# Weighted sums of two attention steps issued together, in every second step

## Chip, cores and metric

The kernel runs on one core of one Trainium2 chip. The metric is the device time of one execution in microseconds; lower is better. TensorE is the matmul engine, VectorE, ScalarE and GpSimd (POOL in the rows) the elementwise ones, SP the queue that issues the transfers.

## What is computed

One transformer layer (16 heads of 16, width 256) followed by a layer of experts, both behind a layernorm, on 4 sequences of 2048 tokens. The part around the change is the attention:

```python
scores = jnp.einsum('bhqd,bhkd->bhqk', q, k) / jnp.sqrt(jnp.float32(HD))
allowed = (idx % STRIDE == 0)[:, None] | (idx[:, None] == idx[None, :])
scores = jnp.where(allowed, scores, -jnp.inf)
attn = jax.nn.softmax(scores, axis=-1)
o = jnp.einsum('bhqk,bhkd->bhqd', attn, v)
```

Only every eighth token (256 of 2048) attends to all keys; each other token sees itself alone, so its result is its own value vector. The attention matrix is therefore computed for 256 queries and 2048 keys a head.

## The kernel before

`build_steps` (lines 81 to 416) writes out one list of steps, `STEPS`. Each engine walks the whole list and issues its own part of each step, so the list is the order of work on every engine, and semaphores tie the engines together. For each of the 4 batches there is a projection stage and an attention stage; behind the last one comes a tail. Next to each stage run "blocks" of the two MLPs (M: the layer's MLP with GELU, F: the experts' with ReLU), eight items a block.

**Attention stage.** Heads go in 8 pairs, keys in 8 groups of 256 (`KK`), which makes 64 steps (`STEPS_B`) a batch. Step 0's scores are issued at the end of the projection stage, so `attention(b)` begins with step 1. `step(s)` (line 309) puts:

- `scores(s)`, "sc" (lines 1720 to 1730): four matmuls of 128 keys by 256 queries for two heads, into PSUM banks 0 and 1. Before them TensorE waits for the exponential of step s - 1, which reads these banks (`bank_free`, line 1631). ScalarE then takes the exponential of 128x1024 elements into one of two `prob` buffers (lines 1146 to 1158); from step 2 on it waits for the weighted sum of step s - 2, which reads the same buffer (line 1156).
- `maxima(s)`, "mx" (lines 1706 to 1715): two matmuls of 512 columns into banks 2 and 3 for the maxima of a head pair that comes later; VectorE reduces them (line 1428). Before them TensorE waits for the reduction of the maxima before (line 1629). They run 12 ahead (`LEAD`), so that steps 52 to 63 have none.
- `weighted(s - 1)`, "at" (lines 1731 to 1741): `prob` times `vals` for two key tiles and two heads, accumulated in bank 4 over the 8 steps of a head pair. Each of the four products is in fp32, with an output of 32 partitions at its own quarter of the array, and the trace shows two matmuls for each: eight a step. It waits for the exponential of its own step. Behind the last one of a head pair stands "or": VectorE copies bank 4 to `oraw` (line 1452).
- `turns(s)` and `moves(s)`: turning `oraw` and the maxima, and transfers for later work.

**Blocks beside it.** A loop over quarters (line 320) puts one quarter of an item after the steps that are due. Part 0 is three up matmuls of 512 columns ("up", 0), part 1 three more ("up", 1), with a fourth in F blocks (line 1809), part 2 six down matmuls of 256 columns ("dn", 0), part 3 "ev" and six more ("dn", 1). `three` (line 1548) issues these products in groups of three (lines 1550 to 1552). ScalarE has GELU or ReLU (lines 1191, 1193) and a rounding copy (line 1199) per item, POOL a subtraction (line 1049). VectorE has, beside the maxima, subtractions for turned tiles (line 1495), the layernorms and the choice of the expert (lines 1342 to 1359).

Batches 0 and 3 have 16 items in the attention stage, so 64 quarters for 64 steps: one quarter a step, and at the stage's start two steps back to back twice (steps 2 and 3, steps 5 and 6). Batches 1 and 2 have 24 items: one quarter behind an odd step, two behind an even one. This is the line that says it:

```python
            ahead = min(2, quarter // 2) if len(blocks) == 2 else 0
            while s < STEPS_B and s * 4 * n <= (quarter + ahead) * STEPS_B:
                step(s)
                s += 1
```

Three places outside wait for the last weighted sum of a batch: SP (line 913) and ScalarE (lines 1124 and 1169).

Of the kernel before, what the change touches and what calls it, by code (L numbers as in the profile page):

```python
# [42 lines left out]
STEPS_B = PAIRS * KK  # L43
# [33 lines left out]
def blocks_of(what, b):  # L77
    return [k for k, s in enumerate(PHASE) if s == (what, b)]


def build_steps():
# [5 lines left out]
    def down(half):  # L87

        if len(pending) <= LAG:
            return  # L90
        i = pending[0]
        put(("dn", i, half))
        if half == 1:
            pending.pop(0)
            if i % FT == FT - 1:
                put(("sum", i // FT))
# [44 lines left out]
    def after(k, f, at):  # L141

        if k < 0:
            return
        what = BLOCKS[k][0]
        if f == 2:
            put(("la", k))
        if what == "M" and f == at:
            put(("lb", k))
        if what == "F" and f in (3, 4):  # L150
            put(("lf", k, f - 3))
        if f == (at + 1 if what == "M" else 5):
            put(("st", k))

    def rows_in(k, f, at):

        if f == (3 if k == 1 else 0) and BLOCKS[k][0] == "M":
            put(("ld", k))
        if f == at and PHASE[k][0] != "tail" and k + 2 < len(BLOCKS) - 1 and BLOCKS[k + 2][0] == "F":
            put(("ld", k + 2))  # L160
# [3 lines left out]
    def mx(b):  # L164
        m = mine[0]
        if m < PAIRS * MPP:
            put(("mx", b, m // MPP, m % MPP))
            mine[0] += 1
            if m % MPP == MPP - 1:
                put(("ng", b, m // MPP))  # L170
# [89 lines left out]
    def attention(b):  # L260
        blocks = blocks_of("attention", b)
        n = FT * len(blocks)

        def scores(s):
            put(("sc", b, s // KK, s % KK))

        def maxima(s):
            if mine[0] < s + LEAD + 1:
                mx(b)

        def weighted(s):
            if s >= 0:
                put(("at", b, s // KK, s % KK))
                if s % KK == KK - 1:
                    put(("or", b, s // KK))

        alone = []

        def turns(s):
            p, kk = s // KK, s % KK  # L280
            if p and kk == 1:
                alone.append([("ot", b, p - 1)])
            if kk == 4 and p + 1 < PAIRS:
                alone.insert(0, [("mt", b, p + 1), ("mtd", b, p + 1)])

        def turned_out(s, taken):

            if alone and (alone[0][0][0] == "mt" or len(blocks) == 2 or s % KK in (0, 7) or not taken):
                for one in alone.pop(0):
                    put(one)  # L290
                return True
            return taken

        def moves(s):
            p, kk = s // KK, s % KK
            if kk == 1 and p and p + 2 < PAIRS:
                put(("kld", b, p + 2))
            if s == 4:
                put(("ldg", b))
            if b + 1 < B:  # L300
                if s == 6 * KK + 1:
                    for q in range(XB):
                        put(("ldx", b + 1, CHUNKS[q]))
                for at, one in ((53, ("pa", b + 1, CHUNKS[0])), (55, ("pb", b + 1, CHUNKS[0])), (58, ("pt", b + 1, CHUNKS[0])),
                                (60, ("pa", b + 1, CHUNKS[1]))):
                    if s == at:
                        put(one)

        def step(s):

            scores(s)
            maxima(s)
            weighted(s - 1)
            turns(s)
            moves(s)

        s, hook = 1, []

        places = [(0, 2, 4, 7)] * 2 if len(blocks) == 2 else [(0, 2, 3, 7), (0, 1, 3, 7), (1, 2, 4, 7)]
        for quarter in range(4 * n):  # L320
# [5 lines that stand above are left out]
            i, part = FT * blocks[0] + quarter // 4, quarter % 4  # L326
            k, f = i // FT, i % FT
            ready = k + 1
            at = places[k - blocks[0]]
            if part == 0:  # L330
                put(("up", i, 0))
            elif part == 1:
                put(("up", i, 1))
                pending.append(i)
                after(k - 1, f, 4)
                rows_in(k, f, 6)
                if f == at[2] + 1:
                    put(("pick", ready, 1))
                if f == at[2] + 2:
                    put(("pick", ready, 3))  # L340
            elif part == 2:
                down(0)
                hook = dict(zip(at, ([("tn", ready, 0)], [("tn", ready, 1), ("xw", ready)], [("ga", ready)], [("pi", ready)]))).get(f, [])
                taken = bool(hook)
                if hook and hook[0][0] == "pi" and alone and alone[0][0][0] == "mt":
                    turned_out(s, False)
                for one in hook:
                    put(one)
                if not hook:
                    taken = turned_out(s, False)  # L350
            else:
                put(("ev", i))
                turned_out(s, taken)
                down(1)
                if f == at[2]:
                    put(("pick", ready, 0))
                if f == at[2] + 1:
                    put(("pick", ready, 2))
        assert s == STEPS_B and not alone
        weighted(STEPS_B - 1)  # L360

    def tail(b):
# [53 lines left out]
    for b in range(B):  # L416
        mine[0] = 0
        projection(b)
        attention(b)
# [1428 lines left out]
```

## Time and profile before

| | |
|---|---|
| median of 3 runs | 1447.2 us (1447.17 to 1449.56) |
| the profiled execution | 1452.35 us |
| its span, first to last instruction | 1450.6 us |
| TensorE (PE) busy | 1404.0 us, 97% |
| VectorE (DVE) busy | 846.5 us, 58% |
| ScalarE (ACT) busy | 721.7 us, 50% |
| GpSimd (POOL) busy | 649.0 us, 45% |
| weighted-sum matmuls, line 1739 | 2048, mean 391 ns |
| exponentials, line 1157 | 256, mean 1023 ns |
| reductions of the maxima, line 1428 | 256, mean 1223 ns |

In rows of the timeline the first number is the start in us from the span's start, the second how long the row lasts. PE is a matmul, PEld a load of weights. Ends of matmuls are modelled and reach over the next one's start; starts are what to go by. A row of several instructions ("x8") lasts from the first start to the last end. In brackets stands the idle time of the engine before it and what ended that. "L1713" is line 1713 of the kernel. The four attention stages last from 163.9 to 310.4, 482.2 to 662, 830.8 to 1010.6 and 1183.9 to 1330.1 us.

### The profile page before, as it was taken

To read this page: it belongs to the slowest core of one execution; us is meant where nothing else is said; L and a number is where in the kernel's file an instruction comes from. 1 tells how busy PE (TensorE), PEld (TensorE's weight loads), DVE (VectorE), ACT (ScalarE), POOL (GpSimd) and SP (SyncE) were. 2 spreads that over 40 slices of the span, in tenths; PEclk is the share of its full clock that TensorE was granted. 3 is DMA by queue.
4 is the path that set the end of the run, shared out by engine and by line. 5 is a ranking of instruction groups with operands and counts; after the bars stand their busy time and mean duration, and the time that the engine had idled before them with its cause. 6 is when DMAs were issued, how large, how long until landed. Compare 5 with 4: busy or idle time off the path is not lost.

```text
span 1450.6 us, 26449 instructions
## 1 busy us (share of the span) xinstructions
PE 1404.0 (97%) x10167; PEld 1063.0 (73%) x10167; DVE 846.5 (58%) x1792; ACT 721.7 (50%) x1071; POOL 649.0 (45%) x533
## 2 busy tenths in 40 slices
PE   6889999999999999999999999999999999999997
PEld 4778655678888766668888866666888875557996
DVE  7747676636656666555647575763566556762332
ACT  3444555554444555554444555555344455555442
POOL 4554321338754414145865431333776441132755
PEclk9899999999999999999999999999999999999999
DMA  7464123215561222212682213220556212310100
GB/s 251 158 177 103 50 51 66 55 41 190 186 163 44 58 59 50 55 44 81 205 211 69 76 31 79 55 55 16 166 188 166 87 38 50 79 26 23 52 15 30
DMA packets 91393, 130.50 MB, mean 90 GB/s; under 512 B 8314, under 2 KB 68180, under 8 KB 88148
## 3 DMA queue, kind: packets, MB, share of 16 engines
q1 hardware_dynamic: 91268, 128.82, 32.2%
q8 instruction: 81, 1.33, 0.4%
q14 instruction: 44, 0.36, 0.1%
HBM read 68.08 MB, written 60.57 MB: 89 GB/s over the span
## 4 chain that ended last, share of the span: by engine, by line
PE 78%; DVE 11%; POOL 5%; issue 2%; ACT 1%; DMA 1%; SPq 0%; POOLq 0%; DVEq 0%; ACTq 0%
PE ps L1550 19%; PE ps L1551 16%; PE ps L1552 16%; PE ps L1739 9%; PE ps L1728 6%; PE ps L1713 4%; DVE mx L1428 3%; PE ps L1787 2%; DVE stats L1302 2%; PE ps L1775 2%; PE ps L1809 2%; POOL rows L1034 2%; PE ps L1745 1%; PE ps L1671 1%; DVE xn L1390 1%
## 5 line engine op out<-in xcount | busy, mean ns | idle before, releaser
L1428 DVE TENSOR_REDUCE mx<-ps 128x2 f32<-128x1024 f32 x256 | 311.1, 1223 | 189.9 <-PE ps L1713 188.3
L1157 ACT ACTIVATE prob<-ps 128x1024 f32<-128x1024 f32 x256 | 261.8, 1023 | 139.1 <-PE ps L1728 138.8
L1049 POOL TENSOR_TENSOR hid1l<-gel,hid1h 128x512 fp32r<-128x512 f32 x85 | 111.3, 1310 | 207.1 <-ACT hid1h L1199 206.9
L1049 POOL TENSOR_TENSOR hid2l<-gel,hid2h 128x512 fp32r<-128x512 f32 x85 | 111.4, 1311 | 201.6 <-ACT hid2h L1199 201.6
L1049 POOL TENSOR_TENSOR hid0l<-gel,hid0h 128x512 fp32r<-128x512 f32 x86 | 112.5, 1308 | 194.2 <-ACT hid0h L1199 194.2
L1191 ACT ACTIVATE gel<-ps,cols 128x512 f32<-128x512 f32 x128 | 88.1, 688 | 181.0 <-PE ps L1552 169.9
L1739 PE MATMUL ps<-prob,vals 128*32 128x256 f32 x2048 | 163.6, 391 | 0.0
L1193 ACT ACTIVATE gel<-ps 128x512 f32<-128x512 f32 x128 | 76.5, 598 | 170.6 <-PE ps L1809 170.6
L1728 PE MATMUL ps<-qslot,kslot 50*128 50x256 f32 x1024 | 128.9, 330 | 1.8 <-ACT prob L1157 1.8
L1728 PEld LDWEIGHTS ps<-qslot,kslot 50*128 50x128 f32 x1024 | 76.2, 184 | 66.5 <-issue 46.9
L1713 PE MATMUL ps<-kslot,qslot 48*128 48x512 f32 x512 | 102.3, 410 | 3.5 <-DVE mx L1428 3.0
L1028 POOL TENSOR_TENSOR rstd<-vare,mhalf 128x4 f32<-128x4 f32 x47 | 48.3, 1027 | 76.7 <-DVE vare L1316 75.0
L1739 PEld LDWEIGHTS ps<-prob,vals 128*32 128x32 f32 x2048 | 40.3, 108 | 57.6 <-issue 50.6
L1034 POOL TENSOR_SCALAR rows<-rows,mv,rstd 128x256 f32<-128x256 f32 x60 | 73.6, 1233 | 0.0
L1550 PE MATMUL ps<-turned0h,wih 128*128 128x512 f32 x128 | 58.7, 459 | 0.0
L1550 PE MATMUL ps<-turned1h,wih 128*128 128x512 f32 x128 | 57.1, 446 | 0.0
L1495 DVE TENSOR_TENSOR turned1l<-ps,turned1h 128x512 fp32r<-128x512 f32 x32 | 22.1, 692 | 59.7 <-ACT turned1h L1164 59.7
L1713 PEld LDWEIGHTS ps<-kslot,qslot 48*128 48x128 f32 x512 | 46.5, 185 | 11.3 <-DVE mx L1428 7.4
L1199 ACT ACTIVATE hid0h<-gel 128x512 fp32r<-128x512 f32 x86 | 54.1, 629 | 1.3
L1550 PE MATMUL ps<-turned1h,w1h 128*128 128x512 f32 x128 | 54.2, 423 | 0.0
L1199 ACT ACTIVATE hid2h<-gel 128x512 fp32r<-128x512 f32 x85 | 53.5, 630 | 1.3
L1199 ACT ACTIVATE hid1h<-gel 128x512 fp32r<-128x512 f32 x85 | 53.4, 629 | 1.3
(244 smaller groups left out, 3956.5 us busy)
## 6 DMA issues: line engine op xcount, KB each, us to landing
k_d<-kst SPq DMA_DIRECT2D x192, 128.0 KB
kslot<-k_d SPq DMA_DIRECT2D x64, 384.0 KB
xin<-in_L_attn_x SPq DMA_DIRECT2D x32, 256.0 KB, 4.0
rows<-xs_d SPq DMA_DIRECT2D x16, 512.0 KB, 6.0
y_d<-rows SPq DMA_DIRECT2D x15, 512.0 KB, 3.1
rows<-y_d SPq DMA_DIRECT2D x15, 512.0 KB, 4.3
out<-rows SPq DMA_DIRECT2D x15, 512.0 KB, 3.9
xs_d<-xin SPq DMA_DIRECT2D x28, 256.0 KB, 2.7
```

Source lines behind the costliest of these rows:

```text
L1034: nc.gpsimd.tensor_scalar(y[:, i, :], y[:, i, :], mv[:, k % 2, i, 0:1], rstd[:, k % 2, i:i + 1], ALU.subtract, ALU.mult).then_inc(final_do ...
L1049: nc.gpsimd.tensor_tensor(hid[i % RING][1][:], gel[i % 2][:], hid[i % RING][0][:], ALU.subtract).then_inc(lo_done, 1)
L1157: nc.scalar.activation(prob[(n - 1) % 2][:].rearrange("p e i q -> p (e i q)"), ps[:, 0:2, :].rearrange("p a n -> p (a n)"), ACT.Exp).then_ ...
L1191: nc.scalar.activation(gel[i % 2][:], ps[:, UP, :], ACT.Gelu, bias=cols[:, B1C + f:B1C + f + 1]).then_inc(act_done, 1)
L1199: nc.scalar.activation(hid[i % RING][0][:], gel[i % 2][:], ACT.Copy).then_inc(hi_done, 1)
L1428: nc.vector.tensor_reduce(best[:, :, j % NQ], ps[:, at:at + 2, :], AX.X, ALU.max).then_inc(maxr_done, 1)
L1550: mm(o, l[0], r[0], start=start, stop=False, skip_group_check=True)
L1551: mm(o, l[0], r[1], start=False, stop=False, skip_group_check=True)
L1552: return mm(o, l[1], r[0], start=False, stop=stop, skip_group_check=True)
L1713: last = mm(ps[:, bank + e, :], qslot[p % SLOTS][half, P * t:P * t + P], kslot[p % SLOTS][half, 512 * piece:512 * piece + 512], start=True ...
L1728: last = mm(ps[:, e, QW * i:QW * i + QW], kslot[p % SLOTS][half, at:at + P], qslot[p % SLOTS][half, :], start=True, stop=True)
L1739: last = mm(ps[at:at + PR, OUT, 0:QW], vals[:, v:v + PR], prob[(n - 1) % 2][:, e, i, :], start=kk == 0, stop=kk == KK - 1)
```

## The change

In `step(s)` the weighted sum of the step before is no longer issued in each step. In even steps the weighted sums of steps s - 2 and s - 1 are issued, one behind the other, after the step's scores and maxima; odd steps issue none. Steps 62 and 63 follow at the end of the stage. Nothing else is changed: the buffers, the waits and the instructions are the same.

```diff
@@ -310,7 +310,9 @@
 
             scores(s)
             maxima(s)
-            weighted(s - 1)
+            if s % 2 == 0:
+                weighted(s - 2)
+                weighted(s - 1)
             turns(s)
             moves(s)
 
@@ -357,6 +359,7 @@
                 if f == at[2] + 1:
                     put(("pick", ready, 2))
         assert s == STEPS_B and not alone
+        weighted(STEPS_B - 2)
         weighted(STEPS_B - 1)
```

## Rows read from the trace of the kernel before

**Rows 1.** The page: TensorE's busy time, and the chain that ended last.
```profile
PE 1404.0 (97%) x10167; PEld 1063.0 (73%) x10167; DVE 846.5 (58%) x1792; ACT 721.7 (50%) x1071; POOL 649.0 (45%) x533
...
PE 78%; DVE 11%; POOL 5%; issue 2%; ACT 1%; DMA 1%; SPq 0%; POOLq 0%; DVEq 0%; ACTq 0%
PE ps L1550 19%; PE ps L1551 16%; PE ps L1552 16%; PE ps L1739 9%; PE ps L1728 6%; PE ps L1713 4%; DVE mx L1428 3%; PE ps L1787 2%; DVE stats L1302 2%; PE ps L1775 2%; PE ps L1809 2%; POOL rows L1034 2%; PE ps L1745 1%; PE ps L1671 1%; DVE xn L1390 1%
```

**Rows 2.** TensorE's idle time before lines 1713 and 1728: releaser, us, times.
```profile
  DVE mx L1428: 10.4, 29
...
  ACT prob L1157: 9.6, 21
```

**Rows 3.** Timeline of batch 0, steps 18 and 19: start, length, engine, line.
```profile
203.10 0.50 PE L1728 MATMUL ps<-qslot,kslot 50*128 50x256 f32 x4
...
203.44 0.39 PE L1713 MATMUL ps<-kslot,qslot 48*128 48x512 f32 x2
203.65 1.02 ACT L1157 ACTIVATE prob<-ps 128x1024 f32<-128x1024 f32 x1 [1.04 <-PE ps L1728]
203.76 0.16 PEld L1739 LDWEIGHTS ps<-prob,vals 128*32 128x32 f32 x8 [0.25 <-issue]
203.76 0.64 PE L1739 MATMUL ps<-prob,vals 128*32 128x256 f32 x8
203.88 1.23 DVE L1428 TENSOR_REDUCE mx<-ps 128x2 f32<-128x1024 f32 x1 [0.92 <-PE ps L1713]
...
204.33 0.50 PE L1550 MATMUL ps<-turned1h,wih 128*128 128x512 f32 x1
...
204.67 0.40 PE L1551 MATMUL ps<-turned1l,wih 128*128 128x512 f32 x1
...
204.91 0.40 PE L1552 MATMUL ps<-turned1h,wil 128*128 128x512 f32 x1
...
205.24 0.50 PE L1728 MATMUL ps<-qslot,kslot 50*128 50x256 f32 x4
```

**Rows 4.** Line 1739's matmuls that run at 204.20: the same sum's second four.
```profile
204.00 0.40 PE L1739 MATMUL ps<-prob,vals 128*32 128x256 f32 x4
```

**Rows 5.** Timeline of TensorE, projection stage of batch 0: maxima straight before a block.
```profile
113.81 0.73 PE L1713 MATMUL ps<-kslot,qslot 48*128 48x512 f32 x4
114.47 0.50 PE L1550 MATMUL ps<-turned1h,w1h 128*128 128x512 f32 x1
114.81 0.40 PE L1551 MATMUL ps<-turned1l,w1h 128*128 128x512 f32 x1
```

**Rows 6.** Timeline of batch 1, steps 45 and 46.
```profile
610.79 0.39 PE L1713 MATMUL ps<-kslot,qslot 48*128 48x512 f32 x2
...
611.22 1.23 DVE L1428 TENSOR_REDUCE mx<-ps 128x2 f32<-128x1024 f32 x1 [1.73 <-PE ps L1713]
...
612.79 0.19 PEld L1713 LDWEIGHTS ps<-kslot,qslot 48*128 48x128 f32 x2
```

**Rows 7.** Timeline of batch 1, steps 7 and 8.
```profile
502.76 0.69 DVE L1495 TENSOR_TENSOR turned1l<-ps,turned1h 128x512 fp32r<-128x512 f32 x1 [0.51 <-ACT turned1h L1164]
...
503.37 1.21 DVE L1428 TENSOR_REDUCE mx<-ps 128x2 f32<-128x1024 f32 x1
...
504.63 0.49 PE L1713 MATMUL ps<-kslot,qslot 48*128 48x512 f32 x2
```

**Rows 8.** Timeline of VectorE, batch 1, between the reductions of steps 12 and 13.
```profile
518.79 1.23 DVE L1428 TENSOR_REDUCE mx<-ps 128x2 f32<-128x1024 f32 x1
519.94 1.11 DVE L1350 TENSOR_TENSOR picke<-picke,pickm 128x32 f32<-128x32 f32 x1
...
521.67 1.22 DVE L1428 TENSOR_REDUCE mx<-ps 128x2 f32<-128x1024 f32 x1
```

**Rows 9.** Timeline of batch 0, steps 61 and 62, without maxima.
```profile
305.22 1.02 ACT L1157 ACTIVATE prob<-ps 128x1024 f32<-128x1024 f32 x1 [0.83 <-PE ps L1728]
...
306.58 0.50 PE L1728 MATMUL ps<-qslot,kslot 50*128 50x256 f32 x4
```

**Rows 10.** Timeline of batch 0, step 6 behind step 5.
```profile
174.70 0.30 PEld L1728 LDWEIGHTS ps<-qslot,kslot 50*128 50x128 f32 x4 [0.80 <-ACT prob L1157]
```

## Prediction

> **What bounds the kernel now.** The page first: TensorE is busy for 97% of the span, and the chain that ended last runs over it for 78% and over VectorE for 11% [rows 1]. So the time is TensorE's own work plus the few places where it stands still. Next, who it waits for: over the whole span the maxima matmuls sat idle 10.4 us for VectorE's reduction (29 times), the score matmuls 9.6 us for ScalarE's exponential (21 times) [rows 2]. Those two loops are what the change reorders around, so next the timeline of one step, then the slack of each loop.
>
> [Rows 3] are step 18 and the start of step 19 of batch 0. From the start of the scores (203.10) the maxima start 0.34 us later, the weighted sum 0.66 later, the block's matmuls (line 1550) 1.23 later, the next scores 2.14 later (205.24). A weighted sum holds TensorE for 0.57 us (203.76 to 204.33).
>
> **What is removed and added.** No instruction, byte or DMA goes or comes. Of the 256 weighted sums the 128 odd ones (and their copy of oraw, line 1452) stay where they were; the 128 even ones move one step later, to just before the odd one. On TensorE they pass the next scores, the next maxima and the one or two quarters between. SP's wait at line 913 and ScalarE's at 1124 and 1169 ask for the last weighted sum of a batch, which is not moved; POOL's queue sees nothing.
>
> **Gain.** A weighted sum is eight matmuls of 128x32 weights. The first four start at 203.76, the other four at 204.00 [rows 3, 4], 0.24 apart; the group then ends with something that is not streaming, as 0.57 less two passes of 0.24 leaves 0.09. After it the first block matmul needs 0.34 to the next one where the one behind it needs 0.24 (204.33, 204.67, 204.91). Does an odd step that goes from maxima straight to the block avoid this? No: maxima to block takes 0.32 (114.15, the last start of the row, to 114.47), with the same 0.34 behind it (114.47 to 114.81) [rows 5], as maxima to weighted sum takes 0.32 (203.44 to 203.76). So an odd step loses exactly 0.57. The even step gains x, the second group behind the first, which no row shows. Nearest is the second pass behind the first within a group: 0.24, so x = 0.48. But 0.024 of that is the first pass's own weight load (durations 0.40 against 0.38), which a second group could hide: then x = 2 x 0.216 = 0.43. Ends: 0.43, and 0.57 if the second group pays all that the first does. I take 0.45, among the near values: 0.12 saved a pair, 128 pairs, **15.4 us** (17.9 at 0.43, 11.5 at 0.48, nothing at 0.57).
>
> What lies in the 0.09 is a drain between forms of the array. The Trainium skill (TensorEngine Tiling (Array Packing), Key Properties) has the rule: a change of tiling mode drains TensorE, a change of tile doesn't. The rows agree; by that rule alone the change would bring all of 11.5 to 17.9 us.
>
> **Cost 1: maxima wait for the reduction.** The step shortened by 0.57 is always the odd one, and between it and the even step there is one quarter in all batches (batches 1 and 2 have two quarters behind an even step, 0 and 3 one). Batch 1, steps 45 and 46 [rows 6]: maxima at 610.79, reduction 611.22 to 612.45, next maxima's weights at 612.79: slack 0.34. The least that any step shows between a reduction's end and these weights is 0.05. Now TensorE is there 0.57 earlier, so it stands for 0.57 + 0.05 - 0.36 (typical slack) = 0.26. Going through the even steps 2 to 50 (25 a batch, later ones have no maxima) in this way:
> - slack 0.34 to 0.37, behind a quarter of 0.9 us: 7 in batches 1 and 2, 3 in 0 and 3: 20 x 0.26 = 5.2 us.
> - a subtraction of 0.69 stands before the odd reduction, as at step 8 of batch 1 [rows 7]: TensorE already meets the reduction's end (504.58, matmuls 504.63), so all 0.57 is lost: 6 x 0.57 = 3.4.
> - slack 0.43 to 0.59, behind the quarter with one more matmul or a late reduction: 0.03 to 0.19 each, 0.35 in batches 0 and 3, 0.65 in 1 and 2: 2.0.
> - slack 0.68 and over: nothing.
> - pairs in which VectorE alone sets the pace (the expert choice, 1.11 us and more between two reductions [rows 8]): they only lose their 0.12, 9 in a batch pair: 18 x 0.12 = 2.2.
>
> **Cost 2: scores wait for the exponential.** It takes 1.02 us and starts 0.55 after the scores [rows 3].
> (a) Even steps: it now also waits (line 1156) for the sum two steps back, which ends at 204.40, not before: start about 204.44, 0.79 later. The next scores come 0.45 later, so 0.34 of slack is used up. Slack there is 0.57 (204.67 to 205.24), 0.51 at least in batches 0 and 3, far more behind two quarters. Margin after the change 0.51 - 0.34 - 0.05 = 0.12: no cost, but little cover. (Without maxima the sum comes 0.23 sooner: 0.11 is used of 0.28 at least, much the same margin.) ScalarE's other work (GELU or ReLU, copy) stands behind it in the queue and is needed one or two quarters later.
> (b) Odd steps, scores without maxima (from step 52 on): exponential 305.22 to 306.24, next scores 306.58 [rows 9], slack 0.34 where 0.57 + 0.05 is wanted: 0.28, twice a batch, 0.07 six times in all: 2.7 us.
> (c) Steps 5 and 6 of batches 0 and 3 run back to back and step 6 already waits for the exponential [rows 10]: 2 x 0.57 = 1.1; steps 2 and 3 likewise, less a wait that it replaces: 0.3.
>
> Sum of costs 5.2 + 3.4 + 2.0 + 2.2 + 2.7 + 1.1 + 0.3 = **16.9 us**. Bounds: about 11 if VectorE, given 0.45 more in every even step, catches up wherever its work doesn't hang on TensorE's; about 20 if every shortfall counts in full.
>
> **Sum.** 16.9 - 15.4 = +1.5 us. Against the profiled execution, 1450.6 of span and 1.75 outside it (1452.35), that is 1453.9; its own time is 5 us over the median, so the median goes from 1447.2 to **1448.7**. A measurement can tell 0.2% (2.9 us) from no change; this is inside.
>
> **Rivals.**
> *Faster: the drain is the price, the waits hardly come.* x = 0.43, costs of 11 or less: -17.9 + 11 = -7, 1440. With no wait at all 1429. For: rows 4 show no gap between passes; reductions late in an odd step may be early once VectorE has the longer even step behind it. Against: from the maxima's start to the next weights a reduction with nothing before it asks for 0.43 + 1.23 + 0.05 = 1.71 us [rows 6], and the odd step would leave 2.00 - 0.57 = 1.43; no catching up helps there. Chance 0.25.
> *Slower: the exponential becomes the bound of the odd step.* Place: scores of odd steps in batches 0 and 3, and of the last steps in all. It decides once the late exponential is over 0.12 later than worked out in (a), as when the two groups run into each other or ScalarE is held by a copy. Price, at 0.15 beyond: 60 steps x 0.15 = 9 us, 1458. Against: ScalarE is idle 1.04 before such an exponential [rows 3]. Chance 0.20.
> *Slower: the second group pays in full.* x = 0.57, no gain: +16.9 less the 2.2 that there is then nothing to lose of, 1461.9. The weights of the second group go to the tiles that the first still uses. Against: all eight loads of one group are in 0.16 after its start [rows 3], while its first matmuls run for 0.40. Chance 0.12. The Trainium skill (TensorE: Matmul & The Clock Gate, What overlaps and what doesn't) says weight loads overlap running matmuls only for another row group; all eight here use all 128 rows, so it speaks for this rival, and the row differs from it. By the rule one more load of 0.11 would be bare in front of each pass, and x would be over 0.57.
> Forecast itself, within 0.2%: 0.38. The remaining 0.05 is slower by a little of everything (costs of 20, x = 0.48: +8.5, 1455.7).
>
> So faster 0.25, the same 0.38, slower 0.37. The range takes in both bounds of the costs and of x but for 0.57 in full: -17.9 + 11 = -7 gives 1440, +8.5 gives 1456; I cut it at 1441 and put it up to 1457 for part of the exponential's case.
>
> **What would show it.** In the changed trace: groups of 16 matmuls of line 1739, about 1.02 from start to the block's next matmul instead of 0.57; the exponential of even steps 1.3 after its scores; the idle time of line 1713 for VectorE up from 10.4 to over 20 us; that of line 1728 for ScalarE up by some 4. Wrong if the 16 take 1.14, if line 1713 waits no more than before, or if odd-step scores wait for the exponential in batches 0 and 3.

## The result, and the profile after

Ten runs of each on the same chips gave 1454.87 us (1450.6 to 1456.07) for the changed kernel and 1449.43 (1446.6 to 1453.08) for the one before: ratio 1.0032, with a 95% interval of 1.002 to 1.0044. It is 4.6 us slower by the ratio, inside the stated range (1441 to 1457) and on the side that had 0.37. The likeliest case, no difference over 0.2%, was not the one that came. The profiled execution took 1454.31 us, 1452.4 of them its span. That is only 1.8 us more span than in the profile before, and the stages at the end of this section show why.

Lines of the kernel are 3 higher in the changed one: 1731 are the scores, 1716 the maxima's matmuls, 1742 the weighted sums, 1160 the exponential, 1431 the reduction. The page, beside [rows 1]:

```profile
PE 1397.6 (96%) x10167; PEld 1079.9 (74%) x10167; DVE 839.0 (58%) x1792; ACT 727.4 (50%) x1071; POOL 648.3 (45%) x533
...
PE 76%; DVE 11%; POOL 5%; issue 3%; ACT 2%; DMA 0%; SPq 0%; POOLq 0%; DVEq 0%; ACTq 0%
PE ps L1553 19%; PE ps L1554 15%; PE ps L1555 15%; PE ps L1742 8%; PE ps L1731 7%; PE ps L1716 4%; DVE mx L1431 2%; PE ps L1790 2%; DVE stats L1305 2%; PE ps L1778 2%; POOL rows L1037 2%; PE ps L1812 2%; PE ps L1748 1%; ACT prob L1160 1%; DVE x1in L1326 1%
...
L1731 PEld LDWEIGHTS ps<-qslot,kslot 50*128 50x128 f32 x1024 | 76.2, 184 | 71.8 <-ACT prob L1160 44.2
L1742 PEld LDWEIGHTS ps<-prob,vals 128*32 128x32 f32 x2048 | 53.8, 110 | 51.2 <-issue 25.7
L1716 PEld LDWEIGHTS ps<-kslot,qslot 48*128 48x128 f32 x512 | 46.3, 185 | 18.1 <-DVE mx L1431 12.2
```

TensorE is busy 6.4 us less in a longer span, and ScalarE has come into the chain with 2% where it had 1%. The idle time before the weights of these three lines was 66.5 (scores), 57.6 (sums) and 11.3 us (maxima) before the change. So the gaps before the sums' weights shrank by 6.4 us, and those before the scores' and the maxima's grew by 5.3 and 6.8. The lines' own waits, beside [rows 2]:

```profile
  DVE mx L1431: 18.8, 39
...
  ACT prob L1160: 49.3, 123
```

The second number is mostly a new name. "issue" ended 46.9 us of the gaps before the scores' weights in the kernel before and ends 17.9 now, and the exponential ends most of the others; what was added is the 5.3 us. The pattern of a step, batch 1, steps 45 and 46, beside [rows 6]:

```profile
609.63 0.39 PE L1716 MATMUL ps<-kslot,qslot 48*128 48x512 f32 x2
...
610.07 1.23 DVE L1431 TENSOR_REDUCE mx<-ps 128x2 f32<-128x1024 f32 x1 [2.17 <-PE ps L1716]
...
610.92 0.30 PEld L1731 LDWEIGHTS ps<-qslot,kslot 50*128 50x128 f32 x4 [0.43 <-ACT prob L1160]
...
611.35 0.18 PEld L1716 LDWEIGHTS ps<-kslot,qslot 48*128 48x128 f32 x2
...
611.77 1.07 PE L1742 MATMUL ps<-prob,vals 128*32 128x256 f32 x16
...
612.54 1.03 ACT L1160 ACTIVATE prob<-ps 128x1024 f32<-128x1024 f32 x1 [1.68 <-PE ps L1742]
...
612.78 0.50 PE L1553 MATMUL ps<-turned0h,wih 128*128 128x512 f32 x1
```

The sixteen matmuls hold TensorE for 1.01 us (611.77 to 612.78) where eight held it for 0.57, so the second group costs 0.44: the gain is there, 0.13 to 0.14 a pair. But the maxima's weights wait for the reduction: it ends at 611.30, they load at 611.35, 1.72 after the maxima before, as worked out (1.71). The late exponential of an even step, and what it leaves, are step 18 of batch 0 and the steps behind it:

```profile
201.62 1.03 ACT L1160 ACTIVATE prob<-ps 128x1024 f32<-128x1024 f32 x1 [1.36 <-PE ps L1742]
...
202.74 0.30 PEld L1731 LDWEIGHTS ps<-qslot,kslot 50*128 50x128 f32 x4 [0.36 <-ACT prob L1160]
```

It ends at 202.65, the scores' weights load at 202.74: 0.09 of slack, 0.05 being the least there is. That margin held.

What had not been foreseen is at step 14 of batches 1 and 2. Timeline of batch 1, steps 13 and 14, beside [rows 8], and below it the share of busy time and the granted clock (the number behind POOL) in five stretches of 3.4 us, two of batch 1 and three of batch 2:

```profile
516.63 1.29 POOL L1052 TENSOR_TENSOR hid0l<-gel,hid0h 128x512 fp32r<-128x512 f32 x1 [4.47 <-ACT hid0h L1202]
516.78 1.18 DVE L1353 TENSOR_TENSOR picke<-picke,pickm 128x32 f32<-128x32 f32 x1
...
518.59 1.23 DVE L1431 TENSOR_REDUCE mx<-ps 128x2 f32<-128x1024 f32 x1
519.87 0.60 PE L1716 MATMUL ps<-kslot,qslot 48*128 48x512 f32 x2 [1.12 <-DVE mx L1431]
520.40 1.93 PE L1742 MATMUL ps<-prob,vals 128*32 128x256 f32 x16
```

```profile
516.70:520.10 3.40, 2.23 (x15) 1.16 (x11) 3.01 (x5) 1.02 (x1) 1.22 (x1) 1.00 0.41 155
520.10:523.50 3.40, 3.40 (x21) 1.64 (x20) 1.72 (x4) 1.02 (x1) 0.00 (x0) 0.50 0.36 96
868.30:871.70 3.40, 2.38 (x15) 1.27 (x13) 3.30 (x5) 1.26 (x2) 1.28 (x1) 1.00 0.33 124
871.70:875.10 3.40, 3.25 (x20) 1.45 (x21) 1.81 (x5) 1.02 (x1) 0.00 (x0) 0.50 0.41 109
875.10:878.50 3.40, 3.40 (x16) 2.99 (x14) 0.00 (x0) 0.60 (x1) 0.00 (x0) 0.50 0.21 77
```

The expert choice sits between two reductions, its operation of 128x32 takes 1.18 us, and TensorE stands for 1.12 us before step 14's maxima. In the kernel before the operation took 1.11 [rows 8], and TensorE stood for 0.48 at this place:

```profile
522.95 0.50 PE L1713 MATMUL ps<-kslot,qslot 48*128 48x512 f32 x2 [0.48 <-DVE mx L1428]
```

TensorE, busy for 2.23 and 2.38 of 3.40 us, then runs at the lower level of its clock, 1.2 of 2.4 GHz, for 3.4 us in batch 1 and 6.8 in batch 2: the sixteen matmuls take 1.93. The attention stages of the kernel before were at 1.00 throughout.

By stage, from the weights of step 1's scores to those of step 63's (first and last start of each row), batches 1 and 2 before, then 0 to 3 after:

```profile
L1728 PEld LDWEIGHTS ps<-qslot,kslot x252: 182/184/187, 485.5 to 660.2; 50*128 50x128 f32 x126
L1728 PEld LDWEIGHTS ps<-qslot,kslot x252: 182/184/188, 834.0 to 1008.8; 50*128 50x128 f32 x126
```

```profile
L1731 PEld LDWEIGHTS ps<-qslot,kslot x252: 182/184/187, 161.5 to 305.6; 50*128 50x128 f32 x126
L1731 PEld LDWEIGHTS ps<-qslot,kslot x252: 182/184/187, 482.1 to 659.6; 50*128 50x128 f32 x126
L1731 PEld LDWEIGHTS ps<-qslot,kslot x252: 182/186/192, 834.1 to 1012.7; 50*128 50x128 f32 x126
L1731 PEld LDWEIGHTS ps<-qslot,kslot x252: 182/184/187, 1186.5 to 1330.3; 50*128 50x128 f32 x126
```

Batches 0 and 3 take 144.1 and 143.8 us where the kernel before took 144.6 and 144.4. Batches 1 and 2 take 177.5 and 178.6 where they took 174.7 and 174.8. The whole loss is in the two batches whose stages have a fall of the clock. The four stages together are 5.5 us longer, but the two spans differ by 1.8. The rest of the span, which the change does not touch, took 812.1 us in the profiled execution before and 808.4 in this one; the clock of the first fell there once more (for 3.4 us, at 13.8).

### The profile page after: what moved, and what is told of

Read it like the earlier page. It is cut to its first block, busy times and chain, and to the rows that moved or that the text cites. A ratio compares the mean times of both kernels' runs of the same rounds, so it can differ in the third digit from the quotient of the medians.

```text
span 1452.4 us, 26449 instructions
## 1 busy us (share of the span) xinstructions
PE 1397.6 (96%) x10167; PEld 1079.9 (74%) x10167; DVE 839.0 (58%) x1792; ACT 727.4 (50%) x1071; POOL 648.3 (45%) x533
## 4 chain that ended last, share of the span: by engine, by line
PE 76%; DVE 11%; POOL 5%; issue 3%; ACT 2%; DMA 0%; SPq 0%; POOLq 0%; DVEq 0%; ACTq 0%
PE ps L1553 19%; PE ps L1554 15%; PE ps L1555 15%; PE ps L1742 8%; PE ps L1731 7%; PE ps L1716 4%; DVE mx L1431 2%; PE ps L1790 2%; DVE stats L1305 2%; PE ps L1778 2%; POOL rows L1037 2%; PE ps L1812 2%; PE ps L1748 1%; ACT prob L1160 1%; DVE x1in L1326 1%
## 5 line engine op out<-in xcount | busy, mean ns | idle before, releaser
L1742 PE MATMUL ps<-prob,vals 128*32 128x256 f32 x2048 | 138.8, 389 | 0.0
L1716 PE MATMUL ps<-kslot,qslot 48*128 48x512 f32 x512 | 106.4, 427 | 7.0 <-DVE mx L1431 6.6
L1742 PEld LDWEIGHTS ps<-prob,vals 128*32 128x32 f32 x2048 | 53.8, 110 | 51.2 <-issue 25.7
```

The lines of the kernel that those rows point to most:

```text
L1716: last = mm(ps[:, bank + e, :], qslot[p % SLOTS][half, P * t:P * t + P], kslot[p % SLOTS][half, 512 * piece:512 * piece + 512], start=True ...
L1742: last = mm(ps[at:at + PR, OUT, 0:QW], vals[:, v:v + PR], prob[(n - 1) % 2][:, e, i, :], start=kk == 0, stop=kk == KK - 1)
```

## The experiments

Theory A, after the result: the pair saves 0.14 us on TensorE; the reduction's wait behind the shortened step takes it back; and the loss comes from the stop at step 14 of batches 1 and 2 with the clock's fall behind it. Rival B: pairs cost everywhere, the late exponential most of all. All ratios are to the kernel before, timed beside each version, with 95% intervals.

In the first four a pointer `nxt` issues all sums up to s - 1 where a condition holds:

```diff
-            if s % 2 == 0:
-                weighted(s - 2)
-                weighted(s - 1)
+            if CONDITION:
+                while nxt[0] < s:
+                    weighted(nxt[0])
+                    nxt[0] += 1
```

**Pairs in batches 0 and 3 only.** CONDITION is `b in (1, 2) or s % 2 == 0`.

> Sums in pairs in batches 0 and 3 only. Theory A (two places at steps 13 to 15 of batches 1 and 2, where VectorE's chain holds the maxima and TensorE's granted clock then halves, make the whole loss; elsewhere the pairing breaks even or gains a little): from the two traces, batch 0 took 0.9 us less and batch 3 0.8 less than before, so this one is 1.7 us faster than before, ratio 0.9988, and no half-clock stretch lies in an attention stage. Rival B (the pairs cost everywhere, the waits for the exponential included): 2 us slower, 1.0015.

1448.89 us against 1449.56, ratio 0.9998 (0.9986 to 1.0009). In its trace no half-clock stretch lies in an attention stage. No loss here: B's 1.0015 is outside the interval. A's 1.7 us are at its edge, so what the pairs bring in these batches is at most little.

**Pairs in batches 1 and 2 only.** CONDITION is `b in (0, 3) or s % 2 == 0`.

> Sums in pairs in batches 1 and 2 only. Theory A: the whole loss is here; from the traces +3.4 and +2.5 us, 5.9 slower than before, ratio 1.0041, with half-clock stretches of 3.4 to 7 us at steps 14 of batches 1 and 2. Rival B: half of the measured loss, 1.0016.

1452.02 us, ratio 1.0019 (1.0008 to 1.0029). The loss is in these batches, but its middle, 2.8 us, is near B's figure, and A's 5.9 (1.0041) is outside the interval. The two parts together make 1.0017 where the whole change had 1.0032; the intervals leave that open. The trace says why the loss can vary. The maxima of step 14 stand for 1.1 us in both batches, as in the change, but the clock does not fall behind them; it falls once, at 640.5, behind step 55:

```profile
518.52:521.92 3.40, 2.24 (x15) 1.15 (x11) 3.02 (x5) 1.02 (x1) 1.22 (x1) 1.00 0.41 155
521.92:525.32 3.40, 3.40 (x31) 2.25 (x29) 1.72 (x4) 1.62 (x2) 0.00 (x0) 1.00 0.34 98
637.10:640.50 3.40, 3.31 (x28) 2.87 (x27) 0.00 (x0) 1.33 (x3) 0.00 (x0) 1.00 0.41 154
640.50:643.90 3.40, 3.40 (x26) 2.04 (x25) 1.08 (x6) 1.11 (x3) 1.29 (x1) 0.50 0.02 5
```

The first stretch holds the stop of step 14 just as the stretch at 516.70 of the changed kernel does, with the same busy time (2.24 against 2.23), and the clock stays up behind it. The fall at 640.5 has 3.31 busy of 3.40 before it. So with the same order of work the fall comes or doesn't, and the busy time just before doesn't tell which. Batch 2, which had none here, shows the price of the pairs without it:

```profile
L1734 PEld LDWEIGHTS ps<-qslot,kslot x252: 182/185/188, 836.1 to 1012.1; 50*128 50x128 f32 x126
```

176.0 us against 174.8 before: 1.2 for the pairs (the longer stop of step 14 among them), and 1.5 and 2.6 more in the two batches of the change that had the fall (177.5 and 178.6).

**The change, with steps 11 to 15 of batches 1 and 2 as before.** CONDITION is `s % 2 == 0 or b in (1, 2) and 11 <= s <= 15`.

> The change, but with steps 11 to 15 of batches 1 and 2 left as before. Theory A: from step 13's scores to step 15's the time falls back from 8.9 and 10.1 us to the 7.0 of before, the half-clock stretches go, and the total is 5 us under the change: ratio to before 0.9995 (0.998 to 1.001). Rival B: these steps are a small part of 62 in each batch, the ratio stays at 1.0025 or more.

1450.34 us, ratio 1.0012 (1.0 to 1.0023). From step 13's scores to step 15's 7.0 us again, and no half-clock stretch in any attention stage. By the ratios 2.9 us of the 4.6 are gone with 5 of 63 steps in two batches (give or take 2.4, as both ratios have their interval), and B's 1.0025 is outside. A is borne out in kind; its 5 us are more than the middle shows. What stays is 1.7 us, with the interval's lower end at none.

**Odd steps in batches 1 and 2.** CONDITION is `b in (0, 3) or s % 2 == 1 or s % KK == 0`.

> Batches 0 and 3 as before; in batches 1 and 2 the pairs come in the odd steps (and the last sum of a head pair alone), so that the shortened step is the even one, which has two quarters behind it. No sum or wait differs in kind. Theory A: 48 pairs that save 0.14 us each and meet neither the reduction (slack over 1 us there) nor the exponential: 6.7 us faster, ratio 0.9955, at least 0.997; line for the maxima's matmuls waits for VectorE about as long as before (10 us) and no clock falls. Rival B (pairing itself costs): 1.000 or slower.

1444.07 us, ratio 0.9963 (0.995 to 0.9976). Here the pair is in the odd step, with one quarter behind, and the shortened even step has two. In the timeline, steps 43 and 44 of batch 1 (scores 1734, maxima 1719, sums 1745, reduction 1434):

```profile
604.87 1.07 PE L1745 MATMUL ps<-prob,vals 128*32 128x256 f32 x16
604.99 1.23 DVE L1434 TENSOR_REDUCE mx<-ps 128x2 f32<-128x1024 f32 x1 [1.04 <-PE ps L1719]
...
606.98 0.50 PE L1734 MATMUL ps<-qslot,kslot 50*128 50x256 f32 x4
...
607.21 0.19 PEld L1719 LDWEIGHTS ps<-kslot,qslot 48*128 48x128 f32 x2
```

The reduction ends at 606.22, a full 0.99 before the next maxima's weights. The same sixteen matmuls, so B is out: a pair pays where the short step is not the one with the short cover. The predicted 0.9955 lies inside the interval. The clock does not fall in any attention stage, as expected; the maxima's matmuls wait 13.0 us for VectorE where about 10 were expected, among them 0.81 us at step 13 of both batches.

**Both together.** Even steps in batches 0 and 3, odd ones in 1 and 2.

> Batches 0 and 3 in pairs in even steps as in the change, batches 1 and 2 in pairs in odd steps. Theory A (a pair saves 0.14 us wherever the shortened step still leaves the reduction its time): the two parts add up, 5.4 us for batches 1 and 2 and 0.3 to 1.3 for 0 and 3: ratio 0.995 to 0.9965. Rival B (batches 0 and 3 break even only by chance of the clock): 0.997 or more.

1442.87 us against 1450.61, ratio 0.9943 (0.9926 to 0.9959). The parts add up, and a little more; it can't be told from the odd steps alone, as the intervals overlap.

**Half the reduction, sums as before, and with pairs.** In both kernels the same line, so that the wait for VectorE goes. The reduction reads 256 of each bank's 512 columns, so these two leave half of the keys out of the maximum:

```diff
-                    nc.vector.tensor_reduce(best[:, :, j % NQ], ps[:, at:at + 2, :], AX.X, ALU.max).then_inc(maxr_done, 1)
+                    nc.vector.tensor_reduce(best[:, :, j % NQ], ps[:, at:at + 2, 0:256], AX.X, ALU.max).then_inc(maxr_done, 1)
```

> The kernel before, with the reduction of the maxima reading 256 of each bank's 512 columns (the maximum is taken over half of the keys; TensorE's work is the same). Theory A: the 10 us for which the maxima's matmuls wait in the kernel before fall to 3 or less: ratio 0.994 to 0.996. Serves as the base for the next one.

> The change, with the same half reduction (maximum over half of the keys). Theory A (the pair saves 0.14 us on TensorE, 17.9 us in all, and it is the wait for the reduction that eats most of it): with that wait gone 5 to 6 us of waits for the exponential remain, so 11 to 13 us less than the kernel before with the half reduction, ratio to that 0.9915 to 0.9925. Rival B (the pair saves little and the loss is the exponential's): no faster than the kernel before with the half reduction.

1442.7 us (0.995, 0.9937 to 0.9963) with single sums, 1437.3 (0.9915, 0.99 to 0.9931) with pairs: a ratio of 0.9965 between them. In both profiles the line of the maxima's matmuls shows no idle time ended by VectorE at all. Then the change is 5 us faster (the two intervals give 2 to 8) instead of 4.6 slower, so the reduction's wait (with what hangs on it, the clock among it) is worth some 10 us. But A had asked for 11 to 13. What eats the rest is in the timeline of the paired kernel, batch 0, step 13:

```profile
189.35 0.69 DVE L1498 TENSOR_TENSOR turned0l<-ps,turned0h 128x512 fp32r<-128x512 f32 x1 [0.94 <-ACT turned0h L1167]
...
190.09 0.27 PE L1721 MATMUL ps<-ident,negs 128*8 128x128 f32 x1 [0.74 <-DVE turned0l L1498]
```

A small transpose (line 1718 of the kernel before, "mt") shares bank 5 with the turned tile before it and waits for that tile's subtraction. It comes in the quarter behind the odd step, so TensorE now stands there for 0.74. The same stop is in the changed kernel at 247.92, where the kernel before had waited 0.18:

```profile
247.92 0.27 PE L1721 MATMUL ps<-ident,negs 128*8 128x128 f32 x1 [0.75 <-DVE turned1l L1498]
```

```profile
250.88 0.27 PE L1718 MATMUL ps<-ident,negs 128*8 128x128 f32 x1 [0.18 <-DVE turned1l L1495]
```

Such stops of 0.74 to 0.75 us stand eight times in the attention stages of the paired kernel with the half reduction, six at line 1721 and two at line 1748 (the turning of oraw), and not in the other: at 0.57 each 4.6 us of the 6 to 8 that were missing.

**The choice one quarter later.** The third part of the choice leaves the odd step's quarter:

```diff
             if part == 0:
                 put(("up", i, 0))
+                if f == at[2] + 2:
+                    put(("pick", ready, 2))
...
                 if f == at[2]:
                     put(("pick", ready, 0))
-                if f == at[2] + 1:
-                    put(("pick", ready, 2))
```

> The change, with the third part of the expert choice (lines 1350 to 1355 of the kernel before) put one quarter later, out of the odd step 13 of batches 1 and 2. There its first operation of 128x32 takes 1.18 us, as it starts just after GpSimd's subtraction, and its reduction comes so late that step 14's maxima stand idle for 1.1 us; the granted clock halves behind it (rows of the changed kernel). Theory A: that stop shrinks below 0.6 us, no half-clock stretch lies there, and the time falls by 2 to 4 us against the change: ratio to before 1.0005 to 1.002. Rival B (the stop only moves to the next maxima, the choice's length is what counts): 1.003 as the change.

> Control: the kernel before with the third part of the expert choice one quarter later, sums as before. Theory A (the move repairs a stop that the change made): the kernel before has there only a stop of 0.5 to 0.8 us in each of batches 1 and 2, so at most 1.5 us faster, ratio 0.999 to 1.0. Rival C (the move is worth the same in any kernel, and says nothing of the change): 0.996 to 0.997, as much as it brought the changed kernel.

The edit acts in all four batches. With pairs 1448.39 us, ratio 0.9993 (0.998 to 1.0007), a little under the 1.0005 to 1.002 that A gave, and B's 1.003 is out; with sums as before 1446.91, ratio 0.9988 (0.9977 to 0.9999). The move is worth 3.9 per thousand (5.6 us, give or take 2.6) in the changed kernel and 1.2 (1.7 us) in the one before, so most of it is the repair of what the change had made, and rival C is out. VectorE's and TensorE's rows at the same place:

```profile
515.33 1.23 DVE L1431 TENSOR_REDUCE mx<-ps 128x2 f32<-128x1024 f32 x1 [0.59 <-PE ps L1716]
516.47 0.18 DVE L1353 TENSOR_TENSOR picke<-picke,pickm 128x32 f32<-128x32 f32 x1
516.61 0.19 PEld L1716 LDWEIGHTS ps<-kslot,qslot 48*128 48x128 f32 x2 [0.20 <-DVE mx L1431]
```

The operation takes 0.18 instead of 1.18, and step 14's maxima load at once behind their reduction. One fall of the clock stayed in this trace, 3.4 us behind step 55 of batch 1 (at 635.6), as in the kernel with pairs in batches 1 and 2 alone. What brings that one wasn't tried.

**The best version, with that move.**

> Pairs in even steps in batches 0 and 3 and in odd steps in batches 1 and 2, and the third part of the choice one quarter later. Theory A: the stops of 0.8 us at step 14 of batches 1 and 2 go: 1 us faster than without the move, ratio 0.9935. Rival B: the same as without it, 0.9943, or worse where the choice now holds another reduction.

1439.71 us against 1450.14, ratio 0.9929 (0.9911 to 0.9947): the fastest that takes the whole maximum, 10.3 us under the kernel before. The stops of 0.8 us, which stand at step 13 and not at step 14 in this version, are still there in its trace:

```profile
517.07 0.49 PE L1719 MATMUL ps<-kslot,qslot 48*128 48x512 f32 x2 [0.83 <-DVE mx L1434]
```

So A's reason failed, though its figure lies in the interval; against the version without the move (0.9943) the time is not told apart.

**The stages in all the traces.** Each is one execution, but a stage that an edit doesn't touch comes out the same to 0.1 us, so this table is finer than the ratios. It has the time from step 1's scores to step 63's, read as above; a star marks a stage with a fall of the clock (3.4 us each, 6.8 in batch 2 of the change).

| kernel | batch 0 | batch 1 | batch 2 | batch 3 |
|---|---|---|---|---|
| before | 144.6 | 174.7 | 174.8 | 144.4 |
| the change | 144.1 | 177.5* | 178.6* | 143.8 |
| pairs in 0 and 3 | 144.1 | 174.8 | 174.8 | 143.7 |
| pairs in 1 and 2 | 144.7 | 177.4* | 176.0 | 144.4 |
| the change but for steps 11 to 15 | 144.2 | 175.3 | 175.4 | 143.7 |
| odd steps in 1 and 2 | 144.7 | 171.1 | 170.8 | 144.3 |
| both together | 144.2 | 171.1 | 170.9 | 143.7 |
| half reduction, single sums | 142.8 | 172.5 | 172.6 | 142.5 |
| half reduction, pairs | 142.0 | 170.6 | 170.7 | 141.6 |
| choice later, pairs | 143.6 | 176.3* | 174.8 | 143.1 |
| choice later, single sums | 144.1 | 173.9 | 173.9 | 143.7 |
| both together, choice later | 143.6 | 171.1 | 170.9 | 143.2 |

Where odd steps have the pairs, one sum of each batch falls behind step 63's scores and out of the count, so 0.57 us a batch of that gain is not one. In the last row the move brings nothing in batches 1 and 2 and 0.5 us in each of the others. With the choice later the pairs cost 0.9 us in batch 2 (174.8 against 173.9) where they cost 1.2 (176.0 against 174.8), both without a fall. So of what the move brings beyond its gain with single sums, the stop's own length is 0.3 us a batch, and the rest is the clock's.

**The clock in all executions.** The traces can't say how often the clock falls, but the mean granted clock of every timed execution can: 0.992 over the ten of the change, 0.994 to 0.995 over the 71 of the kernel before. At two levels that is 23 us at the lower one against 15 to 18 (an estimate, 2 x (1 - clock) x span). Among the executions of one kernel, 1 us more at the lower level goes with 0.42 us more time (a fit over all 166). That puts the clock's part at some 2 to 3.5 of the 4.6 us, the ten taken together.

## Why the prediction was right, point by point

- **The gain.** x was taken at 0.45 and came out at 0.43 to 0.44 (1.01 - 0.57), the near end. The weight loads of the second group run beside the first, as the trace had said and against the Trainium skill's rule for row groups (TensorE: Matmul & The Clock Gate, What overlaps and what doesn't). With 0.43 the gain is 17.9 us instead of 15.4, and the odd step loses its 0.57 in full.
- **Cost 1, the reduction.** The working of a single step held to 0.01 us (1.72 against 1.71). The line's idle time went from 10.4 to 18.8 us, just under the "over 20" that was named, and halving the reduction turned the loss into a gain. Batches 0 and 3 came out 0.5 and 0.6 us ahead; the sum doesn't split all its costs by batch, so no term of it can be set beside that.
- **Pairs in which VectorE sets the pace** were put at 0.12 each, so that such a pair would come out even. This is the term that failed. At step 14 of batches 1 and 2 TensorE stopped for 1.12 us where it had stopped for 0.48, and from step 13's scores to step 15's it took 8.94 us in batch 1 and 10.11 in batch 2, where it had taken 6.95. In the kernel with pairs in batches 1 and 2 the same steps took 7.40 at full clock: the longer stop ate all that the odd step had lost, and the second group's 0.44 came on top, unhidden. The other 1.5 and 2.7 us are the clock's. The prediction had left the clock out: the stop was taken to cost its own length and no more.
- **Cost 2, the exponential.** (a) held: 0.09 of slack was left where 0.12 + 0.05 had been worked out, and no step of batches 0 and 3 with a quarter before it waited for a late one. (b) and (c) came as put, (b) a little smaller: odd steps that were 1.90 long without maxima are 1.62 now, with 0.21 to 0.23 of standing before step 62's scores, and step 6 of batches 0 and 3 waits 0.89 instead of 0.32. Not seen: that the exponential's own length, 0.55 + 1.02 + 0.05, lets no odd step fall under 1.62 where 1.57 was wanted; with full maxima this hides behind the reduction's wait.
- **ScalarE's other work** was costed at nothing as "needed one or two quarters later". In a few places it is needed by the next quarter, with VectorE's subtraction behind it: the transposes that share bank 5. Each lost its 0.57. With the full reduction part of these pairs had been booked as lost anyway.
- **The sum.** +1.5 was said for the work as it stands, with the clock at its level. The stages without a fall say +1.3 (-0.5 and -0.6 in batches 0 and 3, +1.2 in each of 1 and 2, that of batch 1 taken as that of batch 2), so the sum of the waits was right, although single terms of it were not. The change with the choice later is 0.5 per thousand (0.9993 against 0.9988), 0.7 us, slower than its own control, but the intervals reach from 1.8 us faster to 3.2 slower and prove nothing by themselves. The measured +4.6 is the waits and the falls of the clock. The clock was in no term and no rival, and the range reached up to 1457 for the sake of the exponential; that the result lay inside is in this part luck. The rival of the full second group fell by the 1.01, that of the exponential in batches 0 and 3 by the 0.9998 of these batches alone. The rival on the faster side was right in x and wrong in the waits.

## What to carry to other kernels

Moving work from one step to the next makes one step short and one long; look up which of the two has the longer cover behind it, because the same saving gained 5.4 us in one parity and lost in the other. A loop between two engines sets a shortest step (here 0.43 + 1.23 + 0.05 us), and no average load shows it. Where a chain of small operations lies in a step that gets shorter, a stop can cost more than its length, as TensorE's clock may fall behind it: look at the clock of all executions, not of one trace, or move the chain first.

## What the runs showed of the hardware

A VectorE operation with two tensor inputs of only 128x32 takes 0.18 to 0.19 us alone. Started within 0.2 us behind the start of GpSimd's subtraction of 128x512 (1.29 us) it takes 1.1 to 1.3, and ends as that one does: 516.63 + 1.29 = 517.92 against 516.78 + 1.18 = 517.96. So the moment at which ScalarE's copy releases GpSimd decides whether an operation of the choice takes 0.2 or 1.2 us. The Trainium skill (GPSIMD Engine Reference, Specifications) has the two engines share their interfaces to SBUF, with contention for VectorE instructions with two SBUF inputs; the rows agree, and show that the small one waits out the whole of the large one.

The granted clock fell to 1.2 GHz in the middle of stages in which TensorE is busy for 98% (175.96 of 179.80 us), and came back after 3.4 or 6.8 us. It fell behind stretches with 2.23 and 2.38 of 3.40 us busy and behind one with 3.31, and it stayed up behind one with 2.24 and the same stop of 1.1 us. What decides it, these traces don't show. The shorter fall cost 1.5 us and the longer 2.6 (the stages above, less the 176.0 of the one with the stop and no fall), more than the stop.
